# Splitting the low halves of ten expert weight pieces on Pool instead of DVE

## The chip, the cores and the metric

The kernel runs on one core of one Trainium2 chip. The metric is device time in microseconds (us) of one execution; the number given is the median of three runs. The engines are named as in the profile: PE (TensorE), DVE (VectorE), ACT (ScalarE), POOL or Pool (GpSimd), SP (SyncE, which issues all DMAs here).

## What is computed

Four sequences of 512 tokens with 128 channels go through one adaptively modulated block: layer norm, shift and scale; a gated convolution branch with its projections, added back with a gain; a second layer norm, shift and scale; and a mixture of 160 experts of which each token uses 8, plus one shared expert, added back with a gain. Cut to the part that matters here:

```
logits = x @ router_w.T + expert_bias
probs  = sigmoid(logits); top_w, top_idx = top_k(probs, 8)
combine[token, top_idx] = 2.5 * top_w / (sum(top_w) + 1e-9)
h1     = silu(einsum('th,eih->eti', x, w_gate))      # 160 experts, 64 wide
routed = einsum('eti,ehi->th', h1 * combine.T[:, :, None], w_down)
```

All 160 experts are computed for all tokens, and `combine` is zero for those not chosen.

## The kernel before, in words

**Tiling.** A sequence is a chunk (`c` = 0 to 3). Experts go in pairs (2 x 64 = 128 rows), and two pairs make a duo; a chunk has 40 duos, the program 160 (`J` = 40 c + d). Every matmul of the experts is done in fp16 in three parts (`split`, lines 1159 to 1164): high weights by high data, low weights by high data, high weights by low data. So each duo takes 12 matmuls of 512 columns: 6 for the up projection of duo `J` and 6 for the down projection of duo `J - 4`, interleaved by halves.

**The ring of a duo.** PE's `up(J, q)` fills a PSUM bank; ACT's silu (line 803) brings it to `s_all`; DVE multiplies by the combine weights, which a DMA has spread (`gm`, line 1133); ACT writes the fp16 high half (line 822) and DVE the low half, the difference (`lo`, line 1122); PE's down projection of that duo follows. DVE issues `lo(J - 2)` and then `gm(J)` in duo `J`; PE waits for `lo(J - 4)` in duo `J` (line 1411). ACT's silu of duo `J` waits for `lo(J - 4)` too, because it reuses that buffer.

**The weights.** The expert weights come as 20 pieces of 128 x 1024 fp32 (`PIECES`), even ones for up, odd ones for down; a piece serves four duos. A piece is staged by a DMA (`staged(i)`, `w32`), ACT writes `high(i)` = fp16(64 x staged) (`split_hi`, line 687) and DVE writes `low(i)` = 64 x staged - high in one SCALAR_TENSOR_TENSOR (`split_lo`, line 955). The two fp16 halves of piece `i` are written over the staged fp32 of piece `i - 2` (`SHIFT`), so `split_hi(i)` waits until `split_lo(i - 2)` is done (line 686). PE waits for the low half of a piece before the first duo that uses it (lines 1378 and 1413). Pieces 0 to 6 are split before duo 0. The others are split during chunk 0, at places of the table `WITH`:

```
12: ((9, "split_hi"), (2, "hm"), (9, "split_lo"),),
16: ((10, "split_hi"),),
17: ((10, "split_lo"), (11, "split_hi"),),
19: ((1, "ya0"), (11, "split_lo"), (12, "split_hi"),),
```

Piece 13's high half and piece 12's low half are at duo 20, piece 13's low half at duo 22, pieces 14 and 15 at duo 24, 16 and 17 at duo 25 (17's low half at 26), piece 18 at duos 27 and 31, piece 19 at duo 37.

**Order.** `walk` (line 164) runs through one list of steps for all engines; each engine issues its own part of each step in that order and waits on semaphores. So the order on each queue is written out by hand. The steps of the other branch for later chunks (`att`) are mixed into the duos by `WITH`. Pool's own part of the duos is small: one `pow` over 128 x 4 for each of `stat`, `rms` and `rstd2` (lines 610, 613 and 616).

Of the kernel before, what the change touches and what calls it, by code (L numbers as in the profile page):

```python
# [7 lines left out]
ALU = mybir.AluOpType  # L8
# [6 lines left out]
ML = DI // P  # L15
# [309 lines left out]
def build(nc, x, vecs, mats, wmod_d, outT_d, consts, rows, frow_d, symT, rsgT, idf_c, w_d, out):  # L325
# [3 lines left out]
    with ExitStack() as ctx:  # L329
# [97 lines left out]
        def k(name, rows=P):  # L427
# [3 lines left out]
        s = {n: sem(n) for n in (  # L431
            "ld_vec ld_wmod ld_in ld_mat ld_fuse ld_outT ld_cst ld_rows ld_sym0 ld_sym1 wide_set ld_idf ld_mod row_out w_hi w_lo "
            "x_in0 x_in1 x_in2 pool_zero pads zs_zero eps_set one_set scb_set mod_ps mod_half mod_set row_ps row_half row_set "
            "cb_ps cols_ps cb_set gb_set ak_set bm_set fold1 fold1_sb fold2 zb_set wz_hi wz_lo fold3 waf_hi waf_lo "
            "wb_ps wb_set sc_ps sc_hi sc_lo nws_set winf_set win_hi win_lo sym_set wc_hi wc_lo rr_set rsg_hi rsg_lo sdw_set "
            "stats aggr ve_set rstd_set nb_set t1_set h_set hn_set sq_set mse_set rms_set hr_set hnT_ps hnT_set z_ps zh_set zl_set z_mv "
            "conv_ps symb_ps symb_set val_ps tap_set s_set gate_ps gate_set y_ps gy_set wo_set gob_set u_set gx_set base_set o_ps x2_set stats2 aggr2 ve2_set rstd2_set nb2_set "
            "t2_set h2T_ps xh_set x32_set xl_set lg_ps pr_set sh_ps ss_set "
            "mx_set rp_set cw_set sm_set sme_set rs_set cn_set cT_ps cT_set c_out "
            "up_ps s_done gm hi_set lo_set sd_ps dn_ps y_set yT_ps fin out_st"  # L440
# [27 lines left out]
        def pair(J, q, kind):  # L468
# [13 lines left out]
        def _(sp):  # L482
# [16 lines left out]
            sp.dma_start(brow[:], rows.broadcast_to([P, E + D])).then_inc(s["ld_rows"], 16)  # L499
            sp.dma_start(outT[:], outT_d.rearrange("p (m d) -> p m d", m=ML)).then_inc(s["ld_outT"], 16)  # L500
            sp.dma_start(pool_d[:, 2048:2048 + KS * P], symT[:, KS * P:].broadcast_to([P, KS * P])).then_inc(s["ld_sym1"], 16)
# [9 lines left out]
            def setup(n):  # L511
                if n == 20:
                    sp.wait_ge(s["row_set"], 5)
                    sp.dma_start(rowd.rearrange("o (b j) -> (o b) j", b=B - 1), row4[1:B]).then_inc(s["row_out"], 16)
                elif n == 22:
                    sp.wait_ge(s["row_out"], 16)
# [57 lines left out]
        def _(pool):  # L574
# [43 lines left out]
            walk(setup, att, nothing, nothing, nothing, nothing)

        @block.scalar  # L620
        def _(act):
# [10 lines left out]
            def setup(n):  # L632
# [42 lines left out]
                elif n == 8:  # L675
                    act.wait_ge(s["ld_rows"], 16)
                    a(rrtr[0:32], ebias[0:32], ACT.Copy, scale=ES)
                    a(tmp_h[32:64, 2, 0:E], ebias[32:64], ACT.Copy, scale=ES).then_inc(s["rr_set"], 1)
                    act.wait_ge(s["ld_sym1"], 32)
                    a(rsg_h[:], rsg[:], ACT.Copy, scale=ES).then_inc(s["rsg_hi"], 1)  # L680
                    a(sdw[:], sdf[:], ACT.Copy, scale=YS).then_inc(s["sdw_set"], 1)

            def split_hi(i):
                act.wait_ge(ld_w[i], 16)
                if i >= SHIFT:
                    act.wait_ge(s["w_lo"], i - SHIFT + 1)
                a(high(i), staged(i), ACT.Copy, scale=ES).then_inc(s["w_hi"], 1)  # L687

            def att(c, n):
# [97 lines left out]
                elif n == "norm":  # L787
                    act.wait_ge(s["rs_set"], c + 1)
                    act.wait_ge(s["cw_set"], c + 1)
# [52 lines left out]
        def _(dve):  # L842
# [88 lines left out]
            def mod_ready(c):  # L931

                if c:
                    dve.wait_ge(s["ld_mod"], 16)
                else:
                    dve.wait_ge(s["mod_set"], 5)
# [15 lines left out]

            def split_lo(i):
                dve.wait_ge(s["w_hi"], i + 1)
                e.scalar_tensor_tensor(out=low(i), in0=staged(i), scalar=ES, in1=high(i), op0=ALU.mult,  # L955
                                       op1=ALU.subtract).then_inc(s["w_lo"], 1)

            def att(c, n):
# [79 lines left out]
                elif n == "wo":  # L1038
                    dve.wait_ge(s["ld_outT"], 16)
# [5 lines left out]
                    dve.wait_ge(s["ld_rows"], 16)  # L1045
                    if c:
# [18 lines left out]
                elif n == "bn":  # L1065
                    dve.wait_ge(s["x2_set"], c + 1)
                    for t in range(NT):
                        last = e.bn_stats(st2[:, t, :], res[:, c * NT + t, :])
                    last.then_inc(s["stats2"], 1)
                    dve.wait_ge(s["stats2"], c + 1)  # L1070
                    for t in range(NT):
                        last = e.bn_aggr(mv2[:, t, :], st2[:, t, :])
                    last.then_inc(s["aggr2"], 1)
                    dve.wait_ge(s["aggr2"], c + 1)
                    if c:
# [25 lines left out]
                elif n == "cw":  # L1101
                    if c:
# [48 lines left out]
        def _(pe):  # L1151
# [232 lines left out]
            def duo(J):  # L1384
# [12 lines left out]
                for q in range(2):  # L1397
# [96 lines left out]
```

## Time and profile before

| what | value |
|---|---|
| median of 3 runs | 527.46 us (525.43 to 527.53) |
| span of the profiled execution (first to last instruction) | 523.2 us |
| time of a run outside the span, by the median | 4.3 us |
| PE busy | 510.4 us, 98% |
| DVE busy | 492.7 us, 94% |
| ACT busy | 421.3 us, 81% |
| POOL busy | 27.6 us, 5% |
| DVE split of a low half (line 955) | x20, 24.4 us in all |
| ACT split of a high half (line 687) | x20, 20.8 us in all |

Busy time of PE and DVE is a sum of recorded durations, and instructions that follow each other closely overlap in their records: a DVE operation over 128 x 1024 is recorded as 1.22 to 1.24 us, and the next one starts 1.13 to 1.14 us after it. The distance from start to start is what one costs in a full queue. Only the span of the profiled execution is known, not a time of its own; it stands 4.3 us under the median of the runs.

### The profile page before, as it was taken

To read this page: it belongs to the slowest core of one execution; us is meant where nothing else is said; L and a number is where in the kernel's file an instruction comes from. 1 tells how busy PE (TensorE), PEld (TensorE's weight loads), DVE (VectorE), ACT (ScalarE), POOL (GpSimd) and SP (SyncE) were. 2 spreads that over 40 slices of the span, in tenths; PEclk is the share of its full clock that TensorE was granted. 3 is DMA by queue.
4 is the path that set the end of the run, shared out by engine and by line. 5 is a ranking of instruction groups with operands and counts; after the bars stand their busy time and mean duration, and the time that the engine had idled before them with its cause. 6 is when DMAs were issued, how large, how long until landed. Compare 5 with 4: busy or idle time off the path is not lost.

```text
span 523.2 us, 7224 instructions
## 1 busy us (share of the span) xinstructions
PE 510.4 (98%) x2441; PEld 245.8 (47%) x2441; DVE 492.7 (94%) x630; ACT 421.3 (81%) x686; POOL 27.6 (5%) x45
## 2 busy tenths in 40 slices
PE   7989999999999999999999999999999999999996
PEld 5644544445454444444554444444553444444442
DVE  5999999999999999999999999999899799999995
ACT  5488899988999877787799877876799877777774
POOL 5100200004100000000100000000100000000000
PEclk9999999999999999999999999999999999999999
DMA  8897566645364666655455766665463676666650
GB/s 265 301 369 290 179 207 209 199 157 162 122 203 143 237 186 199 200 202 172 162 161 146 232 189 202 202 209 163 134 196 114 219 240 206 206 202 205 201 177 21
DMA packets 33309, 101.88 MB, mean 195 GB/s; under 512 B 3700, under 2 KB 8952, under 8 KB 33272
## 3 DMA queue, kind: packets, MB, share of 16 engines
q1 hardware_dynamic: 33272, 101.43, 60.2%
q8 instruction: 19, 0.31, 0.2%
q14 instruction: 18, 0.15, 0.1%
HBM read 98.52 MB, written 2.36 MB: 193 GB/s over the span
## 4 chain that ended last, share of the span: by engine, by line
PE 69%; DVE 19%; issue 5%; ACT 2%; DMA 2%; POOL 1%; SPq 1%; DVEq 0%; ACTq 0%
PE bank L1162 22%; PE bank L1164 21%; PE bank L1163 21%; DVE g_all L1122 7%; DVE s_all L1133 4%; DVE w L955 2%; PE bank L1309 2%; DMA res<-x_dram 2%; POOL rms L613 1%; PE bank L1319 1%; PE bank L1408 0%; DVE st L965 0%; DVE key L1099 0%; DVE s_all L1129 0%; ACT g_all L822 0%
## 5 line engine op out<-in xcount | busy, mean ns | idle before, releaser
L803 ACT ACTIVATE s_all<-bank 128x512 f32<-128x512 f32 x320 | 189.4, 594 | 69.4 <-PE bank L1164 68.5
L1122 DVE TENSOR_TENSOR g_all<-s_all,g_all 128x1024 f16<-128x1024 f32 x160 | 195.8, 1224 | 13.0 <-ACT g_all L822 12.7
L1133 DVE TENSOR_TENSOR s_all<-s_all,c_all 128x1024 f32<-128x1024 f32 x158 | 193.2, 1223 | 2.4 <-DMA c_all<-combine 2.4
L822 ACT ACTIVATE g_all<-s_all 128x1024 f16<-128x1024 f32 x160 | 168.2, 1052 | 2.1 <-DVE s_all L1133 1.9
L1162 PE MATMUL bank<-x_h,w 128*128 128x512 f16 x320 | 121.3, 379 | 1.0 <-ACT s_all L803 1.0
L1162 PE MATMUL bank<-g_all,w 128*128 128x512 f16 x320 | 121.3, 379 | 0.8 <-DVE g_all L1122 0.7
L1163 PE MATMUL bank<-g_all,w 128*128 128x512 f16 x320 | 121.3, 379 | 0.0
L1164 PE MATMUL bank<-g_all,w 128*128 128x512 f16 x320 | 121.3, 379 | 0.0
L1164 PE MATMUL bank<-x_l,w 128*128 128x512 f16 x320 | 121.3, 379 | 0.0
L1163 PE MATMUL bank<-x_h,w 128*128 128x512 f16 x320 | 121.3, 379 | 0.0
L1162 PEld LDWEIGHTS bank<-g_all,w 128*128 128x128 f16 x320 | 31.3, 98 | 41.0 <-DVE g_all L1122 3.6
L1162 PEld LDWEIGHTS bank<-x_h,w 128*128 128x128 f16 x320 | 31.3, 98 | 40.7 <-ACT s_all L803 4.6
L1163 PEld LDWEIGHTS bank<-g_all,w 128*128 128x128 f16 x320 | 31.3, 98 | 37.8 <-issue 1.3
L1164 PEld LDWEIGHTS bank<-g_all,w 128*128 128x128 f16 x320 | 31.3, 98 | 37.8
L1164 PEld LDWEIGHTS bank<-x_l,w 128*128 128x128 f16 x320 | 31.3, 98 | 37.8
L1163 PEld LDWEIGHTS bank<-x_h,w 128*128 128x128 f16 x320 | 31.3, 98 | 36.0 <-issue 1.3
L1036 DVE SCALAR_TENSOR_TENSOR attw<-bank,vec,attw 128x511 f32<-128x511 f32 (+3 forms) x40 | 29.9, 747 | 0.3
L955 DVE SCALAR_TENSOR_TENSOR w<-w 128x1024 f16<-128x1024 f32 x20 | 24.4, 1226 | 0.2 <-ACT w L687 0.2
L687 ACT ACTIVATE w<-w 128x1024 f16<-128x1024 f32 x20 | 20.8, 1054 | 0.6 <-DVE w L955 0.4
L613 POOL TENSOR_TENSOR rms<-mse,mhalf 128x4 f32<-128x4 f32 x4 | 9.5, 2378 | 197.8 <-DVE mse L977 197.8
L1309 PE MATMUL bank<-attw,wb 128*128 128x512 f32 x32 | 14.7, 592 | 0.0
L616 POOL TENSOR_TENSOR rstd<-ve,mhalf 128x4 f32<-128x4 f32 x4 | 6.7, 1685 | 136.2 <-DVE ve L1077 136.2
(236 smaller groups left out, 376.8 us busy)
## 6 DMA issues: line engine op xcount, KB each, us to landing
c_all<-combine SPq DMA_DIRECT2D x158, 512.0 KB, 4.5
w<-w_dram SPq DMA_DIRECT2D x20, 512.0 KB, 10.1
combine<-cT SPq DMA_DIRECT2D x4, 256.0 KB, 3.1
out_dram<-res SPq DMA_DIRECT2D x3, 256.0 KB, 3.0
s_all<-mats_dram SPq DMA_DIRECT2D x1, 640.0 KB, 6.7
attw<-symT_dram SPq DMA_DIRECT2D x1, 576.0 KB, 8.0
c_all<-symT_dram SPq DMA_DIRECT2D x1, 576.0 KB, 6.6
mod<-rows_mod SPq DMA_DIRECT2D x1, 576.0 KB, 4.4
```

The source lines that it names most:

```text
L613: g.tensor_tensor(rms[:], mse[:], mhalf[:, 0:NT], ALU.pow).then_inc(s["rms_set"], 1)
L687: a(high(i), staged(i), ACT.Copy, scale=ES).then_inc(s["w_hi"], 1)
L803: a(sr[J % SRING][:, q * L:(q + 1) * L], U[q][:], ACT.Silu, scale=1.0 / ES).then_inc(s["s_done"], 1)
L822: a(gh[n % GRING], sr[n % SRING], ACT.Copy).then_inc(s["hi_set"], 1)
L955: e.scalar_tensor_tensor(out=low(i), in0=staged(i), scalar=ES, in1=high(i), op0=ALU.mult, op1=ALU.subtract).then_inc(s["w_lo"], 1)
L1036: e.scalar_tensor_tensor(out=acc[:, t0:t9], in0=val[:, t0 + d:t9 + d], scalar=v("sym_k", mid + d), in1=acc[:, t0:t9], op0=ALU.mult, op1=AL ...
L1122: e.tensor_tensor(gl[n % GRING], sr[n % SRING], gh[n % GRING], ALU.subtract).then_inc(s["lo_set"], 1)
L1133: e.tensor_tensor(sr[J % SRING], sr[J % SRING], cr[J % CRING], ALU.mult).then_inc(s["gm"], 1)
L1162: mm(dst, lh, rh, start=start, stop=False)
L1163: mm(dst, ll, rh, start=False, stop=False)
L1164: return mm(dst, lh, rl, start=False, stop=stop)
L1309: last = mm((A1, A2)[q][:], wb[:, i, q * P:(q + 1) * P], s32[:, i, :], start=False, stop=(i == ML - 1))
```

## The change

For pieces 10 to 19 (`i >= DVELO`) DVE no longer writes the low half. Pool does, in two operations: it multiplies the staged fp32 piece by 64 in place, waits for that on a semaphore of its own (`w_es`), and subtracts the high half, writing fp16. It counts these on a new semaphore `w_lop`, and those that waited for the low half of such a piece (ACT in `split_hi`, PE in `up` and in the down projection) wait for that one. The places in the order stay where they were: Pool now has a part in the `split_lo` steps of `walk`. To make room for the new semaphores some old ones are merged (`ld_outT` into `ld_rows`, `row_out` into `ld_mod`, `stats2` and `aggr2` into `ve2_set`, `sm_set` and `sme_set` into `rs_set`), with the counts waited for raised to match.

```diff
+DVELO = 10
@@
+        def low_ready(engine, i):
+
+            if i < DVELO:
+                engine.wait_ge(s["w_lo"], i + 1)
+            else:
+                engine.wait_ge(s["w_lop"], i - DVELO + 1)
@@ gpsimd
-            walk(setup, att, nothing, nothing, nothing, nothing)
+            def split_lo(i):
+                if i < DVELO:
+                    return
+                pool.wait_ge(s["w_hi"], i + 1)
+                g.tensor_scalar(staged(i), staged(i), ES, None, ALU.mult).then_inc(s["w_es"], 1)
+                pool.wait_ge(s["w_es"], i - DVELO + 1)
+                g.tensor_tensor(low(i), staged(i), high(i), ALU.subtract).then_inc(s["w_lop"], 1)
+
+            walk(setup, att, nothing, split_lo, nothing, nothing)
@@ scalar
                 if i >= SHIFT:
-                    act.wait_ge(s["w_lo"], i - SHIFT + 1)
+                    low_ready(act, i - SHIFT)
@@
-                    act.wait_ge(s["ld_rows"], 16)
+                    act.wait_ge(s["ld_rows"], 32)
@@ vector
             def split_lo(i):
+                if i >= DVELO:
+                    return
@@ tensor
-                    pe.wait_ge(s["w_lo"], 2 * (J // (PER // 2)) + 1)
+                    low_ready(pe, 2 * (J // (PER // 2)))
@@
-                                pe.wait_ge(s["w_lo"], 2 * (d // (PER // 2)) + 2)
+                                low_ready(pe, 2 * (d // (PER // 2)) + 1)
```

## Rows read from the trace of the kernel before

**Rows 1.** The page: span, and the chain by engine.
```profile
span 523.2 us, 7224 instructions
...
PE 69%; DVE 19%; issue 5%; ACT 2%; DMA 2%; POOL 1%; SPq 1%; DVEq 0%; ACTq 0%
```

**Rows 2.** Busy time by stretch: PE, PEld, DVE, ACT, POOL with counts, clock, DMA, GB/s.
```profile
95.00:118.00 23.00, 23.00 (x109) 10.38 (x107) 23.00 (x23) 20.81 (x38) 0.00 (x0) 1.00 0.58 183
118.00:141.40 23.40, 23.40 (x111) 11.72 (x109) 23.16 (x33) 21.21 (x33) 8.36 (x2) 1.00 0.44 138
141.40:164.00 22.60, 22.45 (x120) 11.06 (x120) 22.39 (x35) 22.33 (x39) 0.00 (x0) 1.00 0.57 179
...
240.00:511.00 271.00, 270.04 (x1285) 127.24 (x1284) 254.81 (x286) 216.72 (x340) 4.83 (x3) 1.00 0.59 187
```

**Rows 3.** PE in time (start, duration, what): two steps into a down projection.
```profile
141.10 0.38 PE L1164 MATMUL bank<-x_l,w 128*128 128x512 f16 x1
141.42 0.39 PE L1162 MATMUL bank<-g_all,w 128*128 128x512 f16 x1
...
163.54 0.38 PE L1164 MATMUL bank<-x_l,w 128*128 128x512 f16 x1
164.00 0.39 PE L1162 MATMUL bank<-g_all,w 128*128 128x512 f16 x1
```

**Rows 4.** DVE in time: the low halves of duos 26 and 33.
```profile
140.15 1.22 DVE L1122 TENSOR_TENSOR g_all<-s_all,g_all 128x1024 f16<-128x1024 f32 x1
...
162.73 1.22 DVE L1122 TENSOR_TENSOR g_all<-s_all,g_all 128x1024 f16<-128x1024 f32 x1
```

**Rows 5.** Waits ended by DVE, 141.4 to 165: total us, times, longest.
```profile
PEld bank L1162 <- DVE g_all L1122: 1.6, 3, 0.6
```

**Rows 6.** Line 955: duration ns min/median/max, first and last start.
```profile
L955 DVE SCALAR_TENSOR_TENSOR w<-w x20: 1214/1222/1244, 28.7 to 170.2; 128x1024 f16<-128x1024 f32 x20
```

**Rows 7.** DVE and POOL in time, 119 to 127: one pow of Pool beside DVE's queue.
```profile
118.97 1.24 DVE L955 SCALAR_TENSOR_TENSOR w<-w 128x1024 f16<-128x1024 f32 x1
119.17 6.45 POOL L613 TENSOR_TENSOR rms<-mse,mhalf 128x4 f32<-128x4 f32 x1 [62.34 <-DVE mse L977]
...
122.38 1.24 DVE L1122 TENSOR_TENSOR g_all<-s_all,g_all 128x1024 f16<-128x1024 f32 x1
...
124.65 0.70 DVE L1059 SCALAR_TENSOR_TENSOR attw<-attw,bank 128x512 f32<-128x512 f32 x1
```

**Rows 8.** POOL and DVE in time: the same pow alone, and at one DVE operation.
```profile
249.67 1.01 POOL L613 TENSOR_TENSOR rms<-mse,mhalf 128x4 f32<-128x4 f32 x1 [113.79 <-DVE mse L977]
...
133.97 1.91 POOL L616 TENSOR_TENSOR rstd<-ve,mhalf 128x4 f32<-128x4 f32 x1 [8.35 <-DVE ve L1077]
134.93 1.22 DVE L1133 TENSOR_TENSOR s_all<-s_all,c_all 128x1024 f32<-128x1024 f32 x1
```

**Rows 9.** POOL in time: its only operation over 128 x 1024, one stream.
```profile
1.33 0.95 POOL L583 MEMSET zs<- 128x1024 f16 x1
```

**Rows 10.** Line 1122, all 160: duration ns min/median/max, first and last start.
```profile
L1122 DVE TENSOR_TENSOR g_all<-s_all,g_all x160: 1195/1225/1243, 62.5 to 516.1; 128x1024 f16<-128x1024 f32 x160
```

**Rows 11.** ACT in time: high halves of pieces 10, 12, then 14 and 15.
```profile
98.12 1.06 ACT L687 ACTIVATE w<-w 128x1024 f16<-128x1024 f32 x1
...
105.89 1.06 ACT L687 ACTIVATE w<-w 128x1024 f16<-128x1024 f32 x1
...
122.30 2.00 ACT L687 ACTIVATE w<-w 128x1024 f16<-128x1024 f32 x2
```

**Rows 12.** PE in time: the down projections of duo 22 and duo 36 begin.
```profile
130.95 0.38 PE L1162 MATMUL bank<-g_all,w 128*128 128x512 f16 x1
...
173.08 0.38 PE L1162 MATMUL bank<-g_all,w 128*128 128x512 f16 x1
```

**Rows 13.** DVE in time: piece 19's low half and the low half of duo 36.
```profile
170.19 1.22 DVE L955 SCALAR_TENSOR_TENSOR w<-w 128x1024 f16<-128x1024 f32 x1
171.32 1.23 DVE L1122 TENSOR_TENSOR g_all<-s_all,g_all 128x1024 f16<-128x1024 f32 x1
```

More of the change, by code:

```diff
@@ L431, in build @@
         s = {n: sem(n) for n in (
-            "ld_vec ld_wmod ld_in ld_mat ld_fuse ld_outT ld_cst ld_rows ld_sym0 ld_sym1 wide_set ld_idf ld_mod row_out w_hi w_lo "
+            "ld_vec ld_wmod ld_in ld_mat ld_fuse ld_cst ld_rows ld_sym0 ld_sym1 wide_set ld_idf ld_mod w_hi w_lo w_es w_lop "
             "x_in0 x_in1 x_in2 pool_zero pads zs_zero eps_set one_set scb_set mod_ps mod_half mod_set row_ps row_half row_set "
@@ L436, in build @@
             "stats aggr ve_set rstd_set nb_set t1_set h_set hn_set sq_set mse_set rms_set hr_set hnT_ps hnT_set z_ps zh_set zl_set z_mv "
-            "conv_ps symb_ps symb_set val_ps tap_set s_set gate_ps gate_set y_ps gy_set wo_set gob_set u_set gx_set base_set o_ps x2_set stats2 aggr2 ve2_set rstd2_set nb2_set "
+            "conv_ps symb_ps symb_set val_ps tap_set s_set gate_ps gate_set y_ps gy_set wo_set gob_set u_set gx_set base_set o_ps x2_set ve2_set rstd2_set nb2_set "
             "t2_set h2T_ps xh_set x32_set xl_set lg_ps pr_set sh_ps ss_set "
-            "mx_set rp_set cw_set sm_set sme_set rs_set cn_set cT_ps cT_set c_out "
+            "mx_set rp_set cw_set rs_set cn_set cT_ps cT_set c_out "
             "up_ps s_done gm hi_set lo_set sd_ps dn_ps y_set yT_ps fin out_st"
@@ L499, in _ @@
             sp.dma_start(brow[:], rows.broadcast_to([P, E + D])).then_inc(s["ld_rows"], 16)
[L500 removed]
+            sp.dma_start(outT[:], outT_d.rearrange("p (m d) -> p m d", m=ML)).then_inc(s["ld_rows"], 16)
             sp.dma_start(pool_d[:, 2048:2048 + KS * P], symT[:, KS * P:].broadcast_to([P, KS * P])).then_inc(s["ld_sym1"], 16)
@@ L513, in setup @@
                     sp.wait_ge(s["row_set"], 5)
-                    sp.dma_start(rowd.rearrange("o (b j) -> (o b) j", b=B - 1), row4[1:B]).then_inc(s["row_out"], 16)
+                    sp.dma_start(rowd.rearrange("o (b j) -> (o b) j", b=B - 1), row4[1:B]).then_inc(s["ld_mod"], 16)
                 elif n == 22:
-                    sp.wait_ge(s["row_out"], 16)
+                    sp.wait_ge(s["ld_mod"], 16)
                     sp.dma_start(mod[:, 1:B].rearrange("p b j -> p (b j)"), rowd.broadcast_to([P, (B - 1) * MODC]))\
@@ L787, in att @@
                 elif n == "norm":
-                    act.wait_ge(s["rs_set"], c + 1)
+                    act.wait_ge(s["rs_set"], 3 * c + 3)
                     act.wait_ge(s["cw_set"], c + 1)
@@ L933, in mod_ready @@
                 if c:
-                    dve.wait_ge(s["ld_mod"], 16)
+                    dve.wait_ge(s["ld_mod"], 32)
                 else:
@@ L1038, in att @@
                 elif n == "wo":
-                    dve.wait_ge(s["ld_outT"], 16)
+                    dve.wait_ge(s["ld_rows"], 32)
                     mod_ready(c)
@@ L1068, in att @@
                         last = e.bn_stats(st2[:, t, :], res[:, c * NT + t, :])
-                    last.then_inc(s["stats2"], 1)
-                    dve.wait_ge(s["stats2"], c + 1)
+                    last.then_inc(s["ve2_set"], 1)
+                    dve.wait_ge(s["ve2_set"], 3 * c + 1)
                     for t in range(NT):
                         last = e.bn_aggr(mv2[:, t, :], st2[:, t, :])
-                    last.then_inc(s["aggr2"], 1)
-                    dve.wait_ge(s["aggr2"], c + 1)
+                    last.then_inc(s["ve2_set"], 1)
+                    dve.wait_ge(s["ve2_set"], 3 * c + 2)
                     if c:
@@ L1106, in att @@
                         .then_inc(s["cw_set"], 1)
-                    e.tensor_reduce(sm[:], mx[:], AX.X, ALU.add).then_inc(s["sm_set"], 1)
+                    e.tensor_reduce(sm[:], mx[:], AX.X, ALU.add).then_inc(s["rs_set"], 1)
                 elif n == "sum":
-                    dve.wait_ge(s["sm_set"], c + 1)
-                    e.tensor_scalar(sme[:], sm[:], 1e-9, 1.0 / (ROUTED_SCALE * CS), ALU.add, ALU.mult).then_inc(s["sme_set"], 1)
-                    dve.wait_ge(s["sme_set"], c + 1)
+                    dve.wait_ge(s["rs_set"], 3 * c + 1)
+                    e.tensor_scalar(sme[:], sm[:], 1e-9, 1.0 / (ROUTED_SCALE * CS), ALU.add, ALU.mult).then_inc(s["rs_set"], 1)
+                    dve.wait_ge(s["rs_set"], 3 * c + 2)
                     e.reciprocal(rs[:], sme[:]).then_inc(s["rs_set"], 1)
                     if c == 0:
-                        dve.wait_ge(s["rs_set"], 1)
+                        dve.wait_ge(s["rs_set"], 3)
                         dve.wait_ge(s["cw_set"], 1)
```

3 lines of the change are left out of this document (1 added, 2 removed).

## The prediction, made before the changed kernel was run

> **What bounds the kernel now.** I read the shares of the chain first: PE holds 69% of it and DVE 19% [rows 1]. The busy times by stretch say where: after 240 us PE is busy for all but 1 of 271 us while DVE has room (254.8 us recorded, and its records overlap), but from 95 to 141.4 us both are full [rows 2]. In time, PE starts a matmul of 512 columns every 0.215 us there, and DVE a new operation every 1.13 us. What matters is how early DVE is. The low half of duo 26 starts at 140.15 and takes 1.22 us [rows 4], so it ends at 141.37, and the down projection that needs it starts at 141.42 [rows 3]: 0.05 us later. The low half of duo 33 ends at 163.95 (162.73 plus 1.22 [rows 4]) and PE follows at 164.00 [rows 3], 0.05 us again. So DVE has no reserve at duos 26 and 33, and every microsecond that it loses before them is lost by PE. PE is full afterwards and can't win it back: it goes one to one into the end. The other way there is nearly nothing to win. The steps into those two matmuls are 0.32 and 0.46 us instead of 0.215 [rows 3], and only three waits of PE's weight loads there end on DVE, 1.6 us in all [rows 5], of which the matmul row shows 0.15 us, 22.45 busy of 22.60 [rows 2]. DVE is just in time, not late. The granted clock is 1.00 in all these stretches, and I leave it so [rows 2].
>
> **What is removed.** Ten SCALAR_TENSOR_TENSORs of line 955, recorded at 1.22 us [rows 6]. In the full queue each costs its distance to the next start: 170.19 to 171.32, 1.13 us [rows 13]. Eight of them (pieces 10 to 17) stand at duos 17 to 26 of the table, before the low half of duo 26: 8 x 1.13 = 9.1 us of DVE. Piece 18 lies between duos 26 and 33, piece 19 (at 170.19) behind both.
>
> **What is added.** Twenty Pool operations over 128 x 1024. No row shows either. The nearest is Pool's memset over 128 x 1024, 0.95 us for one stream written [rows 9]. The in-place multiply reads one stream and writes one: at least 0.95 us, at most 2 x 0.95 = 1.9 if they don't overlap; I take 1.0, since a memset already moves one stream at about an element per nanosecond and reading can run beside writing. The subtraction reads two streams and writes one: 1.9 to 2.85 us; I take 2.0. So 3.0 us a piece (2.85 to 4.75).
>
> **What that costs.** If Pool had a path of its own, nothing: it is 5% busy. But the rows say that it hasn't. Pool's pow over 128 x 4 takes 1.01 us when DVE's neighbour reads PSUM for one input [rows 8]. At 119.17 the same pow takes 6.45 us: DVE runs five operations with both inputs in SBUF from 118.97 to 124.65, and Pool ends 0.97 us after 124.65, where DVE begins one that has an input in PSUM [rows 7]. It was held for 5.5 us. At 133.97 it was held for one DVE operation: it ends at 135.88, 0.95 us after DVE's change at 134.93 [rows 8]. So Pool and DVE's two-input SBUF operations exclude each other for something. What the trace doesn't show is the other side. No DVE operation of line 1122 is longer than 1.243 us [rows 10], but Pool's only operations there read four elements. The cost to DVE of a long Pool operation lies between 0 and its full duration. I take the full duration, because the row at 119.17 shows a hold over whole DVE operations, and a path held by one side operation by operation is most simply held so by the other. Up to duo 26 that is 8 x (3.0 - 1.13) = 15.0 us. Six or so DVE steps in that stretch leave the path free (those with a PSUM input over 512 columns, like the one at 124.65 [rows 7], four of 0.60 us from start to start, and the statistics, 1.4 us), 3.8 us in all. Pool holds the path for 24 of some 61 us, so about 1.5 us of them fall beside it: 13.5 us stay. Piece 18 adds 3.0 - 1.13 = 1.9 up to duo 33. Piece 19 adds 1.9 less the reserve of duo 36, whose low half ends at 172.55 (171.32 plus 1.23 [rows 13]) for a matmul at 173.08 [rows 12]: 0.5, so 1.4. Sum: 13.5 + 1.9 + 1.4 = 16.8 us. With 2.85 us a piece it is 15.4, with 4.75 it is 33.
>
> The Trainium skill has the rule for this (SBUF — State Buffer, § Who interferes with whom): a DVE instruction with two SBUF inputs contends with a GpSimd instruction that reads SBUF, and the one that starts first keeps the shared pair for its whole instruction. By that rule, this case's trace agrees for Pool's half (the 5.5 us), and no row shows DVE's half. It speaks against this change: by it the term per piece is Pool's duration less 1.13 us, without it zero. The skill also has a price (GPSIMD Engine Reference, § 3.1 Elementwise — side-by-side cycle accounting): 4497 ns for a Pool tensor_tensor over 2048 fp32, so as an estimate 2.25 us for 1024; with it the sum would be 19 us instead of 16.8.
>
> **The added waits.** ACT's high half of piece i now waits for Pool's low half of i - 2, and behind it on ACT stand silu and the high halves of the duos. Piece 10's high half ends at 99.2 [rows 11]; with one DVE operation (1.13) ahead of each Pool step, its low half is done at 99.2 + 1.1 + 1.0 + 1.1 + 2.0 = 104.4, and ACT wants it at 105.89 [rows 11]: covered by 1.5 us, a stall if Pool is held longer. Piece 13's low half stands behind the pow of 119.17 on Pool's queue. Even if that takes 1.0 us, the low half is done at 123.2 to 125.4, and ACT wants it for piece 15 at 123.3 (second of the two from 122.30 [rows 11]). That is up to 2 us, where DVE is far ahead of PE: the low half of duo 22 ends at 123.62 (122.38 plus 1.24 [rows 7]) for a matmul at 130.95 [rows 12], 7.3 us later. So I cost it at nothing; uncovered it is 2 us. Piece 19: high half from 167.5 to 168.55, low half at 168.6 + 1.1 + 1.0 + 1.1 + 2.0 = 173.8, PE wants it at 173.08 [rows 12]: 0.7 us, inside the 1.4 above. The pow of the second norm (133.97) stands behind pieces 14 and 15 and would end near 135.5; DVE uses it just ahead of the low half at 140.15 [rows 4], so it is covered by 4.6 us. The merged semaphores change no moment: each wait was for things long there, or was at that place before. No DMA is moved, and SP's queue gets nothing.
>
> **Rivals.** (1) Pool gets only what DVE leaves, and DVE isn't held. It needs 9 x 3.0 = 27 us before duo 33. It has the 10.2 us taken from DVE, the 3.8 us above, and some 4.3 us more of one-input steps between 155 and 163 us: 18.3 us. Pool is late by 8.7 us, hands it to ACT through the waits above, and a little more at the start: about +9.5, 537 us. For it: no DVE operation ever got longer [rows 10]. Against: those Pool operations were tiny. (2) No long Pool operation is held nor holds, the 6.45 us being something of pow. Then DVE is relieved and PE loses its three short waits: 0.1 us at the first, 0.25 us at the last [rows 3], at most 0.7 us together. 526.9 us, not slower. It decides if DVE's distance stays 1.13 us beside a Pool multiply and Pool's pair takes near 3 us. Against it stands rows 7. (3) Pool is kept out as at 119.17, again and again. If each of its operations waits for half of those 5.5 us, a piece takes 3.0 + 2 x 2.7 = 8.4 us, eight pieces 67 us, where 42.2 us lie between 99.2 and 141.4. ACT is held at the next high half by the 25 us that are missing; with 3 for the last two pieces +28, 555 us. For it: one hold in the rows is this long [rows 7]. Against: the other is one operation long [rows 8].
>
> **How the numbers follow.** The sum is made on the profiled execution: 523.2 + 16.8 = 540.0 us of span, and 4.3 us around it to the median of 527.46, so 544.2 us. Chances: the forecast 0.50, rival 1 0.17, rival 2 0.13, rival 3 0.15, anything else 0.05. The forecast's own range is 539 (shorter holds than durations) to 558 (the upper price with some of it covered). The range of 8 in 10 takes in rival 1 and most of rival 3: 531 to 558. Left out are rival 2 and times above 558. About 0.5% (2.6 us) is what a measurement can tell from no change. Faster by more would need more than all PE waits there: 0.03. Within it: rival 2 and a little of rival 1, 0.14. Slower: 0.83.
>
> **What would show it.** Line 1122 and line 1133 would have a maximum of 2 to 3.5 us instead of 1.24, or gaps before them, in the stretch of the ten pieces and nowhere else; Pool would show ten multiplies of 1 to 2.2 us and ten subtractions of 2 to 3.2; PE would be idle for some 17 us between 100 and 185 us and as full as now behind. DVE at 1.13 us beside Pool with ACT waiting for Pool at line 687 is rival 1 or, with Pool steps over 4 us, rival 3. I am wrong if a long Pool operation lets DVE through.

## The result

The changed kernel takes 545.15 us (median of 4 runs, 544.88 to 545.37), the kernel before 526.44 us (median of 4, 525.41 to 527.53, on the same chip). The ratio is 1.037, 95% interval 1.035 to 1.039: 18.7 us slower. Forecast were 544.2 us and a range of 531 to 558. In spans the loss is larger, 543.6 - 523.2 = 20.4 us. From this run on, every run has both its time and its span on record, and the time is 1.7 to 2.0 us above the span. So the span of 523.2 belongs to an execution of about 525 us and not to the median of 527.46 that the prediction put beside it.

The profile after, first the page: span, busy time, the chain by engine and the lines that are new or grew.

```profile
span 543.6 us, 7231 instructions
...
PE 517.4 (95%) x2441; PEld 246.5 (45%) x2441; DVE 502.6 (92%) x620; ACT 422.4 (78%) x686; POOL 81.4 (15%) x65
...
PE 67%; DVE 15%; issue 6%; ACT 5%; POOL 4%; DMA 1%; SPq 1%; ACTq 0%; DVEq 0%
...
L630 POOL TENSOR_SCALAR w<-w 128x1024 f32<-128x1024 f32 x10 | 35.1, 3508 | 66.8 <-ACT w L703 66.8
L703 ACT ACTIVATE w<-w 128x1024 f16<-128x1024 f32 x20 | 21.0, 1055 | 11.6 <-POOL w L632 11.2
...
L632 POOL TENSOR_TENSOR w<-w 128x1024 f16<-128x1024 f32 x10 | 23.8, 2384 | 0.8
```

DVE's busy time went up by 9.9 us although ten of its operations are gone. Pool's two groups come to 35.1 and 23.8 us, and ACT, which never waited for Pool ahead of a piece before, waits 11.2 us for it. Line numbers have moved: 1139 and 1150 are now the low half and the product of a duo (1122 and 1133 before), 1179 is the first matmul of `split` (1162), 703 ACT's high half of a piece (687).

Busy time by stretch (columns as in [rows 2]). PE is full behind the stretch of the ten pieces (last row) and has 36.05 us of matmuls in the 46 us from 118 to 164 where it was full before; its granted clock is 0.93 and 0.92 there.

```profile
118.00:141.40 23.40, 19.24 (x82) 10.29 (x80) 18.28 (x23) 11.82 (x19) 17.90 (x8) 0.93 0.35 116
141.40:164.00 22.60, 16.81 (x70) 7.13 (x71) 19.49 (x15) 16.57 (x26) 19.41 (x8) 0.92 0.29 92
...
202.00:260.00 58.00, 58.00 (x270) 26.53 (x269) 57.70 (x58) 45.37 (x70) 0.00 (x0) 1.00 0.63 196
```

DVE and POOL in time in the changed kernel (start, duration, what). DVE's operations over 128 x 1024 with two SBUF inputs, never above 1.244 us before [rows 6, 10], now come in three lengths: 1.21, 2.05 and 3.15 us (and once 1.68, beside the end of a Pool subtraction).

```profile
103.69 2.37 POOL L632 TENSOR_TENSOR w<-w 128x1024 f16<-128x1024 f32 x1
103.99 3.15 DVE L1139 TENSOR_TENSOR g_all<-s_all,g_all 128x1024 f16<-128x1024 f32 x1
106.03 3.75 POOL L630 TENSOR_SCALAR w<-w 128x1024 f32<-128x1024 f32 x1
107.06 2.05 DVE L1150 TENSOR_TENSOR s_all<-s_all,c_all 128x1024 f32<-128x1024 f32 x1
...
109.64 1.21 DVE L1139 TENSOR_TENSOR g_all<-s_all,g_all 128x1024 f16<-128x1024 f32 x1
109.87 2.98 POOL L632 TENSOR_TENSOR w<-w 128x1024 f16<-128x1024 f32 x1
110.78 3.15 DVE L1150 TENSOR_TENSOR s_all<-s_all,c_all 128x1024 f32<-128x1024 f32 x1
...
131.52 2.77 POOL L630 TENSOR_SCALAR w<-w 128x1024 f32<-128x1024 f32 x1
133.31 0.69 DVE L1076 SCALAR_TENSOR_TENSOR attw<-attw,bank 128x512 f32<-128x512 f32 x1 [3.15 <-ACT attw L758]
135.90 1.68 DVE L1139 TENSOR_TENSOR g_all<-s_all,g_all 128x1024 f16<-128x1024 f32 x1 [1.91 <-ACT g_all L838]
...
141.51 0.93 DVE L1094 TENSOR_SCALAR ve<-mv 128x4 f32<-128x4 f32 x1
145.52 1.22 DVE L1139 TENSOR_TENSOR g_all<-s_all,g_all 128x1024 f16<-128x1024 f32 x1 [3.08 <-ACT g_all L838]
```

Beside a busy DVE, a Pool operation here waits for the end of the DVE operation that is under way (the subtraction at 109.87 until 110.78; only the first multiply of the stretch waited for two ends) and then holds the one DVE operation that starts next: the multiply by 0.83 us, the subtraction by 1.93 us. At 131.52 DVE is idle and a multiply takes 2.77 us all the same. A small DVE operation can be held too: the one over 128 x 4 at 141.51, with one input, takes 0.93 instead of 0.17 us and ends with Pool's subtraction.

The waits between 95 and 205 us (engine, line, whom; us in all, times, longest), where before PE had 1.6 us of waits for DVE [rows 5] and ACT none for a piece:

```profile
ACT w L703 <- POOL w L632: 11.2, 4, 5.0
PEld bank L1179 <- ACT s_all L819: 9.3, 10, 4.3
...
DVE g_all L1139 <- ACT g_all L838: 7.5, 6, 3.1
PEld bank L1179 <- DVE g_all L1139: 6.1, 6, 1.7
...
DVE attw L1076 <- ACT attw L758: 3.1, 1, 3.1
...
PE bank L1179 <- POOL w L632: 2.2, 1, 2.2
```

PE in time behind two waits. Behind the second (144.60) the matmuls that were 0.215 us apart are 0.43 us apart, which is the lower of the clock's two levels, 1.2 instead of 2.4 GHz. Eight go at this speed here and eight more at 192.5 us; sixteen extra 0.21 us are 3.4 us. The first row is a third such place: behind PE's wait of 2.6 us for DVE's `attw` sixteen fp32 matmuls take 3.36 us instead of 1.95 in the kernel before, and with the four that follow them some 1.7 us are lost (granted clock 0.75 between 131.3 and 138.0 us). What of this 5.1 us reaches the end is said below.

```profile
134.05 3.36 PE L1336 MATMUL bank<-wo,attw 128*128 128x128 f32 x16 [2.56 <-DVE attw L1076]
...
144.60 0.46 PE L1179 MATMUL bank<-x_h,w 128*128 128x512 f16 x1 [3.83 <-ACT s_all L819]
144.85 0.63 PE L1180 MATMUL bank<-x_h,w 128*128 128x512 f16 x1
145.28 0.63 PE L1181 MATMUL bank<-x_l,w 128*128 128x512 f16 x1
```

**The ledger that the experiments are read with.** For each profiled kernel I took the start of the first down-projection matmul of a duo and subtracted the same moment of the kernel before; from this the same difference at duo 14 is taken off, since no kernel has touched a piece by then (it is between -0.5 and +2.1 us, scatter of what comes before). What is left is the delay in us that PE has gathered up to that duo:

| kernel | duo 17 | 19 | 22 | 24 | 26 | 29 | 33 | 35 | 37 | 45 |
|---|---|---|---|---|---|---|---|---|---|---|
| changed kernel | 0.1 | 3.0 | 7.5 | 13.2 | 14.5 | 16.5 | 16.3 | 16.3 | 20.3 | 20.3 |
| e4, room of three pieces | 0.0 | 3.0 | 3.1 | 7.2 | 9.3 | 13.5 | 13.8 | 13.7 | 22.9 | 23.3 |
| e8, piece 19 back on DVE | 0.1 | 3.0 | 11.0 | 16.2 | 17.5 | 19.5 | 19.3 | 19.3 | 19.3 | 19.3 |
| e5, ten idle multiplies | 0.1 | 2.2 | 2.2 | 2.3 | 4.4 | 5.0 | 5.3 | 5.3 | 5.3 | 5.3 |
| e6, ten idle subtractions | 2.3 | 5.5 | 5.5 | 9.7 | 16.5 | 18.2 | 17.8 | 17.8 | 17.8 | 17.8 |
| e3 (e11), only piece 19 | 0.0 | 0.0 | 0.0 | 0.0 | 0.0 | 0.0 | 0.0 | 0.0 | 7.1 (6.9) | 7.1 (6.9) |
| e9 (e12), with filler | 0.0 | 0.0 | 0.0 | 0.0 | 0.0 | 0.0 | 0.0 | 0.0 | 4.7 (4.7) | 4.7 (4.7) |

The changed kernel's delay comes in three places: 3.0 us at duos 18 and 19, 13.3 us at duos 22 to 29, 4.0 us at duos 36 and 37. Behind that nothing is added and nothing given back, as far as the spans go (543.6 - 523.2 = 20.4).

### The profile page after: what moved, and what is told of

Read it like the earlier page. It is cut to its first block, busy times and chain, and to the rows that moved or that the text cites. A ratio compares the mean times of both kernels' runs of the same rounds, so it can differ in the third digit from the quotient of the medians.

```text
span 543.6 us, 7231 instructions
## 1 busy us (share of the span) xinstructions
PE 517.4 (95%) x2441; PEld 246.5 (45%) x2441; DVE 502.6 (92%) x620; ACT 422.4 (78%) x686; POOL 81.4 (15%) x65
## 4 chain that ended last, share of the span: by engine, by line
PE 67%; DVE 15%; issue 6%; ACT 5%; POOL 4%; DMA 1%; SPq 1%; ACTq 0%; DVEq 0%
PE bank L1179 21%; PE bank L1180 21%; PE bank L1181 21%; DVE g_all L1139 6%; DVE s_all L1150 4%; POOL w L630 2%; PE bank L1326 2%; POOL w L632 2%; DMA res<-x_dram 1%; ACT s_all L819 1%; ACT g_all L838 1%; DVE w L973 1%; PE bank L1336 1%; ACT w L703 1%; PE bank L1425 0%
## 5 line engine op out<-in xcount | busy, mean ns | idle before, releaser
L1139 DVE TENSOR_TENSOR g_all<-s_all,g_all 128x1024 f16<-128x1024 f32 x160 | 202.9, 1268 | 20.4 <-ACT g_all L838 20.1
L1150 DVE TENSOR_TENSOR s_all<-s_all,c_all 128x1024 f32<-128x1024 f32 x158 | 200.4, 1268 | 2.3 <-DMA c_all<-combine 2.3
L630 POOL TENSOR_SCALAR w<-w 128x1024 f32<-128x1024 f32 x10 | 35.1, 3508 | 66.8 <-ACT w L703 66.8
L703 ACT ACTIVATE w<-w 128x1024 f16<-128x1024 f32 x20 | 21.0, 1055 | 11.6 <-POOL w L632 11.2
L632 POOL TENSOR_TENSOR w<-w 128x1024 f16<-128x1024 f32 x10 | 23.8, 2384 | 0.8
L621 POOL TENSOR_TENSOR rms<-mse,mhalf 128x4 f32<-128x4 f32 x4 | 5.0, 1258 | 104.0 <-DVE mse L995 104.0
```

The source lines that it names most:

```text
L630: g.tensor_scalar(staged(i), staged(i), ES, None, ALU.mult).then_inc(s["w_es"], 1)
L632: g.tensor_tensor(low(i), staged(i), high(i), ALU.subtract).then_inc(s["w_lop"], 1)
L1139: e.tensor_tensor(gl[n % GRING], sr[n % SRING], gh[n % GRING], ALU.subtract).then_inc(s["lo_set"], 1)
L1150: e.tensor_tensor(sr[J % SRING], sr[J % SRING], cr[J % CRING], ALU.mult).then_inc(s["gm"], 1)
```

## The experiments

Ratios are to the kernel before, run beside the experiment each time; its median was 524.6 to 525.4 us there. Two theories stand against each other. **Hold**: DVE is held by what Pool reads, and DVE has no reserve. **Chain**: a piece takes Pool so long that ACT (for its next high half) and PE (for piece 19) wait for it.

### e1: the merged semaphores alone

```diff
-DVELO = 10
+DVELO = 20
```

> The whole change but its subject: the merged semaphores stay, all twenty low halves are on DVE again. Every theory says the time of the kernel before, 526.4 us within 0.5%, and DVE operations of at most 1.25 us. Above 529 us some of the loss would belong to the merged semaphores.

Measured: 525.33 us, ratio 1.001 (1.000 to 1.003); the longest low half of a duo on DVE is 1.226 us. The merged semaphores cost nothing that can be told; all of the loss comes with the operations that were moved.

### e2: the relief alone

This kernel leaves out the low halves of pieces 10 to 19; PE takes the high half in their place.

```diff
-            return high(i, at, P), low(i, at, P)
+            return high(i, at, P), (low if i < DVELO else high)(i, at, P)
@@ low_ready
-                engine.wait_ge(s["w_lop"], i - DVELO + 1)
+                engine.wait_ge(s["w_hi"], i + 1)
@@ gpsimd, split_lo
-                pool.wait_ge(s["w_hi"], i + 1)
-                g.tensor_scalar(...)
-                pool.wait_ge(s["w_es"], i - DVELO + 1)
-                g.tensor_tensor(...)
+                return
```

> Leaves out the low halves of pieces 10 to 19 altogether (PE uses the high half in their place), on DVE and on Pool: only the relief of DVE by 10 x 1.13 = 11.3 us is left. Theory of the prediction: DVE was just in time, not late, so at most 0.7 us are won: 525.7 us. Rival, DVE was the true bound between 95 and 164 us: up to 9 us won, 517 to 520 us.

Measured: 525.11 us, ratio 1.001 (1.000 to 1.002). In the profile PE gains 0.6 us, by duo 35, as the three short waits of [rows 3, 5] promised; in the time even that can't be told. Even if Pool's part had cost nothing, the change could have won nothing that a measurement tells. Busy time by stretch of e2 (columns as in [rows 2]) shows the other side: DVE has 39.7 us of work between 95 and 141.4 where it had 46.2, and PE is as full as it was.

```profile
95.00:141.40 46.40, 46.40 (x219) 22.28 (x218) 39.70 (x48) 42.07 (x69) 2.01 (x2) 1.00 0.51 170
```

### e5, e6, e7: Pool's operations with nobody waiting for them

All three start from e1 and add to Pool, at the places of the ten pieces, one operation on tiles that nothing waits for (`xa`, the first 1024 fp32 of `wc_l`, idle by then; the subtraction also reads piece 1's high half and writes a tile of its own, `xc`); DVE keeps all its work, and no engine waits for Pool's result.

```diff
-                if i < DVELO:
+                if i < 10:
                     return
                 pool.wait_ge(s["w_hi"], i + 1)
-                ...
+                if i > 10:
+                    pool.wait_ge(s["w_es"], i - 10)
+                g.tensor_scalar(xa, xa, 1.0, None, ALU.mult).then_inc(s["w_es"], 1)          # e5
+                g.tensor_tensor(xc[:], xa, high(1), ALU.subtract).then_inc(s["w_es"], 1)     # e6
+                g.memset(xc[:], 1.0).then_inc(s["w_es"], 1)                                  # e7
```

> The kernel before (with the merged semaphores) plus ten Pool multiplies over 128 x 1024 fp32 on a tile that nothing else uses then, started at the same places as in the change; nobody waits for them and DVE keeps all its work. Theory 'hold': each holds one DVE operation by 0.84 us, so DVE loses 9 x 0.84 = 7.6 us up to duo 33, where it has no reserve: 532 to 533 us. If only waits for Pool cost time: 525.3 us, unchanged.

> The same with ten Pool subtractions (fp32 less fp16 to fp16, 128 x 1024) for the multiplies. Theory 'hold': 1.94 us each, 9 x 1.94 = 17.5 us up to duo 33 and about 1.4 more at duo 36: 542 to 545 us. If only waits for Pool cost time: 525.3 us. If the hold were over the instruction whatever it reads, multiplies and subtractions would cost in the ratio of their durations alone (2.77 to 2.12 us), not 0.84 to 1.94.

> The same with ten Pool memsets (fp16, 128 x 1024, 0.95 us each), which write and read nothing. If only Pool's reads hold DVE: no DVE operation above 1.25 us and 525.3 us. If writes hold too: 0.8 to 0.9 us each, 532 us.

Measured: e5 531.21 us, ratio 1.013 (1.011 to 1.014), 5.3 us of delay at duo 33. e6 543.60 us, ratio 1.037 (1.035 to 1.039), 17.8 us at duo 33. e7 525.46 us, ratio 1.001 (1.000 to 1.003), no delay, and no low half of a duo above 1.226 us. Ten subtractions alone, which nobody waits for, cost as much as the whole change. DVE in e6, held by two subtractions in a row (start, duration, what):

```profile
101.25 1.21 DVE L1152 TENSOR_TENSOR s_all<-s_all,c_all 128x1024 f32<-128x1024 f32 x1
102.39 3.15 DVE L1141 TENSOR_TENSOR g_all<-s_all,g_all 128x1024 f16<-128x1024 f32 x1
105.46 3.15 DVE L1152 TENSOR_TENSOR s_all<-s_all,c_all 128x1024 f32<-128x1024 f32 x1
108.53 1.21 DVE L975 SCALAR_TENSOR_TENSOR w<-w 128x1024 f16<-128x1024 f32 x1
```

So for these three operations the hold goes with what Pool reads: two streams 1.93 us, one stream 0.83, none 0. It doesn't go by the duration, which for the multiply is 2.77 us. (Each number of streams was tried with one kind of operation only, so kind and streams aren't told apart.) e5 came out 2.3 us under its expectation because only six of the nine multiplies up to duo 33 held a DVE operation. In e6 some twenty matmuls are 0.43 us apart, but they cost little: DVE's low half of duo 33 is 17.1 us late, its lengthened operations add up to 16.7 us and its idle time to 0.5, and PE follows that low half by 0.72 us where it was 0.05. So at most 0.7 of the 17.8 us is the clock's. The last multiply of e5 shows the other direction, POOL in time:

```profile
173.34 16.88 POOL L634 TENSOR_SCALAR wc_l<-wc_l 128x1024 f32<-128x1024 f32 x1 [24.22 <-ACT w L705]
```

DVE's queue kept it out for 14 us, a dozen of its operations. Nobody waited for it, so it cost nothing.

### e10: the same pair by itself, behind the end

`xa` and `xc` are the tiles of e5 and e6.

```diff
+            pool.wait_ge(s["fin"], B + 1)
+            for r in range(4):          # 0, 1 alone; 2 beside two SBUF inputs; 3 beside a PSUM input
+                if r >= 2:
+                    pool.wait_ge(s["w_lop"], r - 1)
+                g.tensor_scalar(xa, xa, 1.0, None, ALU.mult).then_inc(s["w_es"], 1)
+                pool.wait_ge(s["w_es"], 2 * r + 1)
+                g.tensor_tensor(xc[:], xa, high(1), ALU.subtract).then_inc(s["w_es"], 1)
+                pool.wait_ge(s["w_es"], 2 * r + 2)
@@ vector, behind the end
+            dve.wait_ge(s["w_es"], 4)
+            for r in range(12):
+                o = e.tensor_tensor(low(2 + r), sr[r % SRING], gh[r % GRING], ALU.subtract)
...
+            for r in range(18):
+                o = e.tensor_tensor(high(2 + r // 2, r % 2 * L, L), Y[:], gh[r % GRING][:, 0:L], ALU.subtract)
```

> The kernel before (with the merged semaphores) and behind its end a measurement by itself, which adds some 50 us: Pool's multiply and subtraction twice with DVE idle; then beside twelve DVE operations with two SBUF inputs of 128 x 1024; then beside eighteen of 128 x 512 with one input in PSUM. From the changed kernel: alone 2.8 and 2.1 us; beside two SBUF inputs DVE has one operation longer by 0.84 and one by 1.94 us, and Pool's take up to 3.8 and 3.0; beside a PSUM input neither holds the other, DVE stays at 0.69 us and Pool at 2.8 and 2.1.

Measured: one execution, 560.43 us, of which only the stretch behind the end is used. POOL and DVE in time there:

```profile
525.89 2.79 POOL L641 TENSOR_SCALAR wc_l<-wc_l 128x1024 f32<-128x1024 f32 x1
528.76 2.12 POOL L643 TENSOR_TENSOR xc<-wc_l,w 128x1024 f16<-128x1024 f32 x1
533.44 3.60 POOL L641 TENSOR_SCALAR wc_l<-wc_l 128x1024 f32<-128x1024 f32 x1 [2.56 <-DVE w L1178]
537.12 2.38 POOL L643 TENSOR_TENSOR xc<-wc_l,w 128x1024 f16<-128x1024 f32 x1
548.75 2.77 POOL L641 TENSOR_SCALAR wc_l<-wc_l 128x1024 f32<-128x1024 f32 x1 [9.25 <-DVE w L1183]
551.60 2.12 POOL L643 TENSOR_TENSOR xc<-wc_l,w 128x1024 f16<-128x1024 f32 x1
...
530.91 16.47 DVE L1178 TENSOR_TENSOR w<-s_all,g_all 128x1024 f16<-128x1024 f32 x12 [10.20 <-POOL xc L643]
547.31 10.84 DVE L1183 TENSOR_TENSOR w<-bank,g_all 128x512 f16<-128x512 f32 x18
```

Twelve DVE operations 1.13 us apart with 1.22 for the last take 13.7 us; they took 16.47, so the pair held DVE for 2.8 us, the sum of 0.83 and 1.93 again. Beside DVE operations with one input in PSUM Pool takes 2.77 and 2.12 us as if alone, and the eighteen take 10.84 us, 0.60 each, as in the kernel before. All as expected. It also gives the price that the prediction had to guess: alone, a piece costs Pool 2.8 + 2.1 = 4.9 us, not 3.0.

### e4: take ACT's wait away

```diff
-SHIFT = 2
+SHIFT = 3
@@ to make room
-        row4 = sb("row4", [B, MODC])
+        row4 = cT0[0:B, 0:MODC]
```

> The changed kernel with SHIFT = 3: a piece is split over the staging place of the piece three before it, so ACT waits for Pool's low half of i - 3 and not i - 2 (a small early tile shares memory with a later one to make room). Theory 'chain' (ACT waits for Pool, PE idles and then runs at the lower clock; the shift grows by 10 us at duos 22 to 24): those waits of 11.2 us fall to under 3 and the time to about 535 to 537 us. Theory 'hold' (DVE has to carry 27.8 us of holds for 11.3 us taken away, whoever waits for whom): the time stays at 542 to 545 us, since DVE then loses at duo 26 what it loses now in waits.

Measured: 549.37 us, ratio 1.048 (1.043 to 1.052). Both theories missed the total (535 to 537 and 542 to 545 us), because piece 19 got worse: POOL in time, and the wait that it made (us in all, times, longest).

```profile
184.36 8.89 POOL L630 TENSOR_SCALAR w<-w 128x1024 f32<-128x1024 f32 x1 [20.32 <-ACT w L703]
```

```profile
PE bank L1179 <- POOL w L632: 6.6, 1, 6.6
```

The multiply came in only at the sixth end of a DVE operation, at 190.5 us.

Up to duo 35 the run tells more. The edit didn't take all of ACT's waits for Pool away: of 11.2 us in four waits one of 4.9 us is left, ahead of piece 17. The delay at duo 24 falls from 13.2 to 7.2 us; but at duo 29 it is 13.5 against 16.5, and at duo 33 13.8 against 16.3. Of the 6 us won at duo 24, 3.5 are lost again by duo 33. "Hold" had 14.9 us by then (9 x 1.65) and the run has 13.8; what "chain" would have won with the last wait gone as well, this run doesn't show.

### e3 and e8: piece 19, alone and left out

```diff
 e3: -DVELO = 10
     +DVELO = 19
 e8: -            if i < DVELO:
     -                engine.wait_ge(s["w_lo"], i + 1)
     +            if i < DVELO or i == PIECES - 1:
     +                engine.wait_ge(s["w_lo"], min(i, DVELO) + 1)
```

(and in e8 the matching condition in both `split_lo`).

> Only piece 19 goes to Pool. Theory 'hold': Pool's two operations hold DVE for 0.84 and 1.94 us, 2.78 in all, less 1.13 taken away, less 0.5 us of reserve at duo 36: +1.1 us, 527.6. Theory 'chain': Pool needs 6.1 us for a piece, and the down projection of duo 36 waits for it directly, as in the changed kernel, where the shift grows by 4.0 us there: +4, 530.4 us, with a wait of PE on Pool of about 2 us.

> The changed kernel with piece 19 back on DVE (pieces 10 to 18 on Pool). In the changed kernel the shift against the kernel before grows by 4.0 us at duos 36 and 37, which the ledger puts down to piece 19 (PE waits for Pool 2.2 us, eight matmuls follow at the lower clock). If the parts add up, the time is that of the changed kernel less 4.0: 541 us. If other delays take the place of this one: 544 to 545 us.

Measured: e3 531.79 us, ratio 1.014 (1.012 to 1.016): one piece costs 7.2 us. POOL and DVE of e3 in time:

```profile
169.07 6.55 POOL L630 TENSOR_SCALAR w<-w 128x1024 f32<-128x1024 f32 x1 [32.76 <-ACT w L703]
175.70 2.36 POOL L632 TENSOR_TENSOR w<-w 128x1024 f16<-128x1024 f32 x1
...
169.49 1.22 DVE L1150 TENSOR_TENSOR s_all<-s_all,c_all 128x1024 f32<-128x1024 f32 x1
170.62 1.22 DVE L1139 TENSOR_TENSOR g_all<-s_all,g_all 128x1024 f16<-128x1024 f32 x1
171.76 1.21 DVE L1150 TENSOR_TENSOR s_all<-s_all,c_all 128x1024 f32<-128x1024 f32 x1
172.89 2.05 DVE L1139 TENSOR_TENSOR g_all<-s_all,g_all 128x1024 f16<-128x1024 f32 x1
```

The multiply came in only at the fourth end of a DVE operation, at 172.89. PE waits 4.5 us for Pool and runs twelve matmuls 0.43 us apart. Here "chain" is right and its size was still too small.

e8: 545.18 us, ratio 1.038 (1.036 to 1.041): 4 us above 541, what it should be if the parts add up, and near the 544 to 545 of the other case. The ledger shows that piece 19's part did go (19.3 us at duo 35, 19.3 at 45), but 3 us more had gathered by duo 24. The first row that differs is Pool's pow that stands ahead of piece 13: 1.94 us in the changed kernel, here

```profile
126.15 5.35 POOL L621 TENSOR_TENSOR rms<-mse,mhalf 128x4 f32<-128x4 f32 x1 [5.25 <-DVE mse L995]
```

kept out until DVE's operation with a PSUM input at 130.53, with ACT's longest wait for Pool now 8.0 us instead of 5.0. So the parts don't add up: which end of a DVE operation lets Pool in isn't fixed by the program alone. The runs of these kernels scatter accordingly, e4 from 546.3 to 552.2 and e8 from 543.7 to 547.0 us.

### e9, e11, e12: what the lower clock costs

```diff
+                            if n == 36:
+                                pe.wait_ge(s["cT_set"], 4)
+                                for _ in range(22):
+                                    mm(A3[:], rsg_h[:, 0:P], x_h[1][:])
                             if c == 0 and d % (PER // 2) == 0:
                                 low_ready(pe, 2 * (d // (PER // 2)) + 1)
```

> The kernel with only piece 19 on Pool (531.8 us, where PE idles 4.7 us ahead of the down projection of duo 36 and then runs twelve matmuls at 0.43 us instead of 0.215), with 22 matmuls whose result nobody reads in that place: 22 x 0.215 = 4.7 us of work in the idle time. If the idle time lets the clock fall, the twelve run at 0.215 us: 2.5 us less, 529.3 us. If the clock falls for another reason, 531.8 us or, if the filler is late itself, a little more.

> Only piece 19 on Pool once more, beside the next one and the same runs of the kernel before, because the two were timed on different occasions (531.8 and 531.5 us, each with a spread of some 2 us) while their profiles differ by 2.3 us at duo 37. Both theories: 531 to 532 us.

> The same with the 22 matmuls in PE's idle time. If the clock costs what the profile shows (twelve matmuls at 0.43 us instead of 0.215), 2.3 to 2.5 us less than only piece 19 on Pool: ratios to the kernel before of about 1.014 and 1.010. If the clock's loss is given back elsewhere, equal ratios.

Measured: e9 531.50 us, ratio 1.011 (1.007 to 1.015). e11 532.72 us, 1.015 (1.012 to 1.018); e12 531.27 us, 1.012 (1.009 to 1.014). PE of e12 in time: it works through the wait, and the matmuls behind are 0.215 us apart.

```profile
174.85 4.91 PE L1432 MATMUL bank<-x_h,rsg_h 128*128 128x512 f16 x22
179.60 0.38 PE L1179 MATMUL bank<-g_all,w 128*128 128x512 f16 x1
179.82 0.38 PE L1180 MATMUL bank<-g_all,w 128*128 128x512 f16 x1
```

In both pairs of profiles the wait is 4.7 us with and without filler, and the 2.2 to 2.4 us behind it are gone with filler. The medians go the same way by 0.3 and 1.5 us (e3 and e9 were run on different occasions; by the ratios 1.3 and 1.6 us), but the intervals overlap: the clock's cost is shown in the traces and not told apart in the time.

## Why the prediction was right, and where it wasn't

The mechanism held: Pool's operations hold DVE, DVE has no reserve, and PE can't win it back. That the forecast fell within 1 us of the measured time is luck. In spans 16.8 us were forecast and 20.4 came; 2.5 of the missing 3.6 us were given back by the 4.3 us around the span, which the later runs show to be 1.8. Within the 16.8, too much hold and no idle time nearly cancelled, as the terms show.

**What bounds it** was right: DVE just in time for PE, PE full behind, so a delay goes one to one into the end and relief wins nothing. e2 shows that relief wins nothing (ratio 1.001); e6 shows that a delay of DVE is lost by PE (17.1 and 17.8 us at duo 33) and stays to the end.

**Relief of 10 x 1.13 us** was right as a term.

**Pool's prices** were wrong for one of the two: the multiply takes 2.77 us alone and not 1.0, above even the upper bound of 1.9 that I built from the memset [rows 9]. The memset was no guide to an operation that reads and computes. The subtraction takes 2.12 us, I took 2.0.

**The hold over the full duration** was wrong for the multiply (0.83 of 2.77 us) and nearly right for the subtraction (1.93 of 2.12). The sum 2.76 us a piece stands close to my 3.0 only because a price too low met a share too high.

**The added waits at nothing** was wrong, and it is the largest error. I had Pool's low half of piece 12, the pow and piece 13 follow each other with 3.0 us a piece; with 4.9 us alone and some 6 beside DVE, ACT waited 11.2 us for Pool at its high halves. Behind the two long ones of these waits (5.0 us, ended at 131.64, and 4.9, ended at 142.51) ACT's `attw` and high halves of duos came late, and DVE stood idle for 3.15 + 1.91 + 3.08 = 8.1 us up to duo 24, in which Pool's operations held nobody.

**Why the sum held all the same** can be read on DVE. Up to duo 33 the lengthened operations of the changed kernel add up to 18.0 us (seven by 0.83, five by 1.93, and three by 0.46, 0.76 and 1.33, each against its length before), where I had 27 less 1.5. 18.0 less 10.2 of relief plus 8.1 of idle time, 0.2 of which was there before, are 15.7 us; the low half of duo 33 is 16.1 us later (179.06 against 162.73 [rows 4], less 0.2 at duo 14). I had 13.5 + 1.9 = 15.4: 7.5 us too much of hold, 7.9 too little of idle time. The same count, made on the other kernels from duo 14 to the low half of duo 33, comes within 0.7 us of what is measured:

| kernel | DVE lengthened | DVE idle | taken off DVE | sum, less the 0.2 | low half of duo 33 later by |
|---|---|---|---|---|---|
| changed kernel | 18.0 | 8.1 | 10.2 | 15.7 | 16.1 |
| e4 | 20.0 | 3.5 | 10.2 | 13.1 | 13.8 |
| e8 | 17.1 | 12.0 | 10.2 | 18.7 | 19.2 |
| e5 | 4.9 | 0.0 | 0 | 4.7 | 5.3 |
| e6 | 16.7 | 0.5 | 0 | 17.0 | 17.1 |

Holds and waits take each other's place in part: e4 has 4.6 us less idle time than the changed kernel and 2.0 us more of hold.

**Piece 19 at 1.4 us** was wrong: 4.0 in the changed kernel and 7 alone. In the changed kernel each Pool step did have at most one DVE operation ahead of it, as assumed:

```profile
185.53 3.70 POOL L630 TENSOR_SCALAR w<-w 128x1024 f32<-128x1024 f32 x1 [24.37 <-ACT w L703]
189.32 2.38 POOL L632 TENSOR_TENSOR w<-w 128x1024 f16<-128x1024 f32 x1
...
191.85 0.38 PE L1179 MATMUL bank<-g_all,w 128*128 128x512 f16 x1 [2.15 <-POOL w L632]
```

The pair took 6.2 us where I had 5.2 (1.9 more for the prices, 1.0 less for the waits ahead of them), and the high half ended 4.1 us and not 4.5 ahead of PE's need; so PE waited for Pool 2.2 us, not 0.7, and lost 1.7 more by the clock. In e3 and e4 the other assumption fails too, "one DVE operation ahead of each Pool step": there it was four and six. That long keeping-out was rival 3, and [rows 7] had shown it for the pow; I used it for a rival and left it out of the sum where only 0.7 us of cover was missing.

**The clock left at 1.00** was wrong: 5.1 us of PE's time in three places. Only the 1.7 us behind duo 36 add to the end. The 3.4 us before lie where PE then waits for DVE in any case: at duo 33 DVE's holds and idle time give 15.7 of 16.1 us, and PE follows the low half by 0.19 us where it was 0.05.

**The rivals.** Rival 2 (no exclusion) fell with the first 3.15 us. Rival 1 (DVE never held) fell with the same rows. Rival 3 is not the mean but true in places. The tell-tales named ahead came out: DVE maxima of 2.05 and 3.15 us and only in this stretch, Pool's subtractions 2.1 to 3.0 us. Three didn't: the multiplies take 2.8 to 4.2 us, not 1 to 2.2; ACT waits for Pool as well; and PE is idle for 11.6 us between 95 and 185, not some 17, since the lower clock takes a part.

**What holds whom.** The Trainium skill (SBUF — State Buffer, § SBUF: two separate sides and § Who interferes with whom) says that the one that starts first keeps the shared pair for its whole instruction. These traces agree that a DVE operation is held and that Pool's reading is what holds it: e7's fills hold nothing, and DVE with a PSUM input isn't held (e10). They don't agree on the whole instruction: the multiply takes 2.77 us and holds 0.83. The measurement decides. The price in the Trainium skill (GPSIMD Engine Reference, § 3.1 Elementwise — side-by-side cycle accounting), 4497 ns for 2048 elements and so by estimate 2.25 us for 1024, is near the 2.12 us measured.

**What stays open**: what decides which end of a DVE operation lets Pool in (the first, the fourth, the sixth, one after a dozen), why the multiply holds DVE for less than a third of its duration, and whether the hold goes by the streams read or by the kind of operation.

## What to carry to other kernels

Before work is moved from DVE to Pool, count DVE's neighbours that have both inputs in SBUF: beside them a Pool operation holds DVE by an amount that has to be measured (here 0.83 us for a multiply that reads one stream of 1024 and 1.93 for a subtraction that reads two), against the 1.13 us that one DVE operation did in one pass, and Pool's result comes late by as many DVE operations as happen to keep it out. Ask first whether the relieved engine is late or just in time: where PE follows DVE by 0.05 us and is full behind, relief is worth nothing and a hold ahead of that place is worth its length. A time around the span that doesn't come from the same execution can hide an error of the sum: here 2.5 us. And price a wait that appears on a third engine by Pool's whole time beside a busy DVE, not by its time when DVE is idle.

## What the runs showed of the hardware that I had not expected

A Pool multiply over 128 x 1024 fp32 in place takes longer (2.77 us) than a subtraction of two streams into fp16 (2.12 us), but holds DVE for less (0.83 against 1.93 us). A Pool operation can be kept out by a full DVE queue for 14 us (e5, 16.88 us in all) and is let in at the next end in other places. PE's granted clock fell to the lower level behind waits of 2.2 us (after three matmuls), 2.6 and 3.8 us in the changed kernel, 4.5 in e3 and 6.6 in e4, and stayed there for eight to thirteen matmuls of 512 columns; behind one wait of 3.3 us in e4 (PE at 141.52) it didn't fall. So a wait can cost more than its length: at piece 19 2.3 us became 4.0 in the changed kernel and 4.7 became 7.1 in e3, while with matmuls in the wait (e9, e12) the clock stayed at the upper level. Where PE waits for DVE soon afterwards, as in e6, the lower clock costs next to nothing.
